# Relaying q, k and v through memory in runs of 64 floats instead of 16

## The reference

```
n  = layernorm(x)
q, k, v = n @ Wq.T, ctx @ Wk.T, ctx @ Wv.T      # each 16 heads x 16 channels, per token
attn = softmax(q . k * 0.25)                    # 16 x 16 head-by-head scores of one token
o  = attn . v, laid out as (head, token, channel) and read back as rows of 256
x  = x + o @ Wp.T + bp
x  = x + moe(layernorm(x)) + shared_ffn(layernorm(x))   # 16 experts, the best 2 per token
```

## Time and profile before

| what | us |
|---|---|
| median of three runs | 1795.53 (1794.02 to 1797.23) |
| the profiled execution | 1800.4 |
| its span | 1798.6 |
| PE busy | 1513.8 (84% of the span) |
| DVE busy | 1326.2 (74%) |
| POOL busy | 1315.4 (73%) |
| ACT busy | 726.7 (40%) |

### The profile page before, as it was taken

How to read it: one execution, slowest core, us unless ns; L and a number is a source line. 1 busy time by engine, 2 the same in 40 slices (tenths; PEclk the granted TensorE clock), 3 DMA queues, 4 the chain that set the end, 5 groups by cost and what they waited for, 6 DMA issues and landing times.

```text
span 1798.6 us, 50791 instructions
## 1 busy us (share of the span) xinstructions
PE 1513.8 (84%) x17109; PEld 1320.3 (73%) x17110; DVE 1326.2 (74%) x3378; ACT 726.7 (40%) x1346; POOL 1315.4 (73%) x1253
## 2 busy tenths in 40 slices
PE   4699999999999999999999999976677676676774
PEld 4578888888878887888888888855566666665774
DVE  6677889787999899988998999875455555455553
ACT  3344454445444544454445444422133332233231
POOL 4277787778787877878787878767567777677676
PEclk9799999999999999999999999987788988889887
DMA  8788888888898889888988898845877765777773
GB/s 219 151 191 174 175 164 228 184 181 164 212 199 173 173 207 199 176 175 182 224 176 178 186 212 175 151 166 210 259 216 215 223 210 165 216 210 228 210 216 91
DMA packets 945835, 344.76 MB, mean 192 GB/s; under 512 B 824088, under 2 KB 898730, under 8 KB 940288
## 3 DMA queue, kind: packets, MB, share of 16 engines
q1 hardware_dynamic: 892464, 166.19, 51.7%
q0 software_dynamic: 33600, 92.91, 14.0%
q10 hardware_dynamic: 19728, 85.13, 13.0%
HBM read 200.37 MB, written 148.15 MB: 194 GB/s over the span
## 4 chain that ended last, share of the span: by engine, by line
PE 31%; issue 17%; SPq 16%; DVE 13%; another core or an unknown queue 7%; POOL 6%; DMA 5%; ACT 4%; DVEq 0%; POOLq 0%; ACTq 0%
SPq L276 6%; SPq L281 5%; SPq L289 4%; PE bank_z L1460 4%; PE bank_a L1193 3%; PE bank_y L1180 2%; PE bank_y L1178 2%; PE bank_a L1332 2%; PE bank_y L1179 2%; ACT xn L645 2%; PE bank_z L1178 2%; DMA w_sb<-q_dram 2%; DMA kv_dram<-w_sb 2%; PE bank_z L1180 2%
## 5 line engine op out<-in xcount | busy, mean ns | idle before, releaser
L410 POOL DMA_INDIRECT slots<-xn,slot_i x256 | 279.4, 1091 | 98.2 <-issue 55.0
L1132 DVE SCALAR_TENSOR_TENSOR v_area<-bank_y,tail,v_area 128x256 f32<-128x256 f32 x288 | 121.6, 478 | 155.6 <-PE bank_y L1180 68.2
L531 POOL DMA_INDIRECT sums<-v_area,tail x144 | 147.1, 1022 | 65.3 <-issue 33.5
L1178 PE MATMUL bank_y<-w_hi,xn_hi 128*128 x288 | 98.8, 343 | 110.9 <-POOL xn_lo L523 79.6
L531 POOL DMA_INDIRECT out<-v_area,tail x144 | 147.5, 1024 | 52.9 <-issue 35.6
L722 ACT ACTIVATE th<-bank_z 128x512 f32<-128x512 f32 x72 | 43.0, 598 | 297.5 <-PE bank_z L1460 141.1
L1178 PEld LDWEIGHTS bank_y<-w_hi,xn_hi 128*128 128x128 f32 x288 | 59.5, 206 | 127.6 <-issue 127.2
L419 POOL DMA_INDIRECT sums<-v_area,slot_i x128 | 128.1, 1000 | 33.2 <-issue 29.8
L1178 PE MATMUL bank_y<-wsh_out_hi,hid_hi 128*128 128x256 f32 x512 | 143.0, 279 | 1.3 <-POOL hid_lo L441 1.3
L1180 PE MATMUL bank_y<-wsh_out_hi,hid_lo 128*128 128x256 f32 x512 | 142.8, 279 | 0.0
L1179 PE MATMUL bank_y<-wsh_out_lo,hid_hi 128*128 128x256 f32 x512 | 142.7, 279 | 0.0
(11 more groups left out here) (229 smaller groups left out, 5381.1 us busy)
## 6 DMA issues: line engine op xcount, KB each, us to landing
k_area<-slots SPq DMA_DIRECT2D x288, 129.0 KB
v_area<-sums SPq DMA_DIRECT2D x288, 128.0 KB
kv_dram<-w_sb ACTq DMA_DIRECT2D x32, 1024.0 KB
x_sb<-in_x_in SPq DMA_DIRECT2D x32, 512.0 KB
ctx_sb<-in_ctx_t SPq DMA_DIRECT2D x32, 512.0 KB
q_dram<-q_sb ACTq DMA_DIRECT2D x32, 512.0 KB
k_area<-kv_dram SPq DMA_DIRECT2D x256, 64.0 KB
w_sb<-q_dram SPq DMA_DIRECT2D x256, 64.0 KB
```

The lines of the kernel that those rows point to most:

```text
L410: pool.indirect_dma_start(slots[j], bass.IndirectOffsetOnAxis(ap=slot_i[:, par, j, i:i + 1], axis=0), row_of[j][:, i, :], None).then_inc(S ...
L531: pool.indirect_dma_start(target, bass.IndirectOffsetOnAxis(ap=tail[:, r, t, 1 - j:2 - j].bitcast(u32), axis=0), y_ring[:, r, t, :], None, ...
L1132: st = nc.vector.scalar_tensor_tensor(out=y_ring[:, r, t, :], in0=Y[t // 2][:, t % 2 * C:(t % 2 + 1) * C], scalar=tail[:, r, t, j:j + 1], ...
L1178: mm(out, lhs_hi, rhs_hi, start=start, stop=False)
```

## The change

A run of four tokens of one batch now lies side by side, so that a piece of the relay is 64 floats, 256 bytes.

- A projection tile takes every fourth token: token `4 p + i` comes out on partition p of tile i. The stationary side of the projections is therefore read with a step of four floats, 16 bytes. `x_sb` is loaded to match, with four DMAs in place of one.
- ScalarE writes the tiles interleaved: k and v as `(16, 4, 16)`, so that each run of 16 floats is followed by that of the next token; q as `(256, 4)`, so that neighbouring floats belong to neighbouring tokens and each copy writes with a step of 16 bytes.
- k and v have a DRAM tensor each. k and q are stored by four DMAs each, of 32 partitions, which put the rows in the order that the reads want; v is stored by one.
- The 24 reads have 16 pieces per partition, of 64 floats. `k_diag` and `v_diag` have the eighth outside of the token. q stays interleaved, so the stationary side of the score matmuls (32 columns) is read with a step of 16 bytes.
- The waits count the new numbers of DMAs: 80 for k and v in place of 16, 64 for q, 64 for x.

```diff
@@ sync
+            def load_x_in(c):
+                rows = x_in[c].rearrange("(m t) i f -> i m t f", t=BPC)
+                for i in range(BPC):
+                    sp.dma_start(x_sb[32 * i:32 * i + 32, :, :], rows[i]).then_inc(S["x_in_done"], 16)
...
-                sp.wait_ge(S["kv_stored"], at(16, c, 16))
+                sp.wait_ge(S["kv_stored"], at(80, c, 80))
                 for src, t in eighths:
                     rows = slice(16 * t, 16 * t + 16)
-                    sp.dma_start(k_diag[rows, :, t % 4, :],
-                                 kv[src, :, :, 0, :].rearrange("n i (d g) -> d (n i) g", d=D)).then_inc(S["qk_read"], 16)
-                sp.wait_ge(S["q_stored"], at(16, c, 16))
+                    sp.dma_start(k_diag[rows, t % 4, :, :].rearrange("d (n a) g -> d n (a g)", a=BPC), k[src]).then_inc(S["qk_read"], 16)
+                sp.wait_ge(S["q_stored"], at(64, c, 64))
                 for src, t in eighths:
                     rows = slice(16 * t, 16 * t + 16)
-                    sp.dma_start(q_rows[rows, :, t // 4 * H:(t // 4 + 1) * H],
-                                 q[src].rearrange("n i (d h) -> d (n i) h", d=D)).then_inc(S["qk_read"], 16)
+                    sp.dma_start(q_rows[rows, :, t // 4, :], q[src]).then_inc(S["qk_read"], 16)
...
@@ scalar
+            def store_by_eighth(dram, rows, done):
+                by_i = dram.rearrange("(t i n) f -> i t n f", t=8, i=BPC)
+                for i in range(BPC):
+                    act.dma_start(by_i[i], rows[32 * i:32 * i + 32, :]).then_inc(S[done], 16)
...
-                    nc.scalar.activation(kv_sb[:, i, :], KV_BANKS[i][:, :], ACT.Copy).then_inc(S["kv_out"], 1)
+                    nc.scalar.activation(kv_by_tile[:, i], KV_BANKS[i][:, :].rearrange("p (w o f) -> p w o f", w=2, f=H),
+                                         ACT.Copy).then_inc(S["kv_out"], 1)
-                act.dma_start(kv_dram[c], kv_sb).then_inc(S["kv_stored"], 16)
+                store_by_eighth(k_dram[c], kv_sb[:, 0:BPC * C], "kv_stored")
+                act.dma_start(v_dram[c], kv_sb[:, BPC * C:]).then_inc(S["kv_stored"], 16)
...
-                        st = nc.scalar.activation(q_sb[:, t, :], Q_BANKS[i][:, j * C:(j + 1) * C], ACT.Copy, scale=ln1_rstd[:, t:t + 1])
+                        st = nc.scalar.activation(q_by_tile[:, t], Q_BANKS[i][:, j * C:(j + 1) * C], ACT.Copy, scale=ln1_rstd[:, t:t + 1])
-                act.dma_start(q_dram[c], q_sb[:, :, :]).then_inc(S["q_stored"], 16)
+                store_by_eighth(q_dram[c], q_sb[:, :], "q_stored")
@@ tensor, scores
-                            m = (u * 8 + n) * BPC + QUARTER_OF[a]
-                            last = mm(SCORE_BANKS[u][32 * a:32 * a + 32, n * 4 * H:(n + 1) * 4 * H], q_rows[:, m, :],
-                                      k_diag[:, m, :, :].rearrange("p t g -> p (t g)"), start=True, stop=True)
+                            row, tile = QUARTER_OF[a] * 4 + u * 2 + n // 4, n % 4
+                            m = row * BPC + tile
+                            last = mm(SCORE_BANKS[u][32 * a:32 * a + 32, n * 4 * H:(n + 1) * 4 * H], q_by_row[:, row, tile, :],
+                                      k_diag[:, :, m, :], start=True, stop=True)
@@ tensor, project
-                        tokens = slice(i * P, (i + 1) * P)
+                        tokens = slice(i, TOK, BPC)
```

More of the change, by code:

```diff
@@ L59, in xattn_ffn_kernel @@
         q_dram = nc.dram_tensor("q_dram", [CHUNKS, P, BPC * C], f32).ap()
-        kv_dram = nc.dram_tensor("kv_dram", [CHUNKS, P, BPC * 2 * C], f32).ap()
+        k_dram = nc.dram_tensor("k_dram", [CHUNKS, P, BPC * C], f32).ap()
+        v_dram = nc.dram_tensor("v_dram", [CHUNKS, P, BPC * C], f32).ap()
         slots = [nc.dram_tensor(f"slots{j}", [NO_TILE + P, ROW], f32).ap() for j in range(TOP)]
@@ L95, in xattn_ffn_kernel @@
         ctx_sb = sb("ctx_sb", [P, KT, TOK])
-        q_sb = sb("q_sb", [P, BPC, C])
+        q_sb = sb("q_sb", [P, BPC * C])
+        q_by_tile = q_sb[:, :].rearrange("p (f i) -> p i f", i=BPC)
         w2_sb = sb("w2_sb", [P, E * C])
-        kv_sb = w2_sb[:, 0:BPC * 2 * C].rearrange("p (i f) -> p i f", i=BPC)
-        q_rows = w2_sb[:, BPC * 2 * C:].rearrange("p (m h) -> p m h", h=32)
+        kv_sb = w2_sb[:, 0:BPC * 2 * C]
+        kv_by_tile = kv_sb.rearrange("p (w o i f) -> p i w o f", w=2, i=BPC, f=H)
+        q_rows = w2_sb[:, BPC * 2 * C:].rearrange("p (n c f) -> p n c f", c=2, f=BPC * H)
+        q_by_row = w2_sb[:, BPC * 2 * C:].rearrange("p (n f i) -> p n i f", i=BPC, f=2 * H)
         k_area = sb("k_area", [P, GROUPS * P])
         v_area = sb("v_area", [P, GROUPS * P])
-        k_diag = k_area[:, 0:GROUPS * 4 * H].rearrange("p (m t g) -> p m t g", m=GROUPS, t=4)
-        v_diag = v_area[:, 0:GROUPS * 4 * D].rearrange("p (m t d) -> p m t d", m=GROUPS, t=4)
+        k_diag = k_area[:, 0:GROUPS * 4 * H].rearrange("p (t m g) -> p t m g", m=GROUPS, t=4)
+        v_diag = v_area[:, 0:GROUPS * 4 * D].rearrange("p (t m d) -> p t m d", m=GROUPS, t=4)
         w1_sb = sb("w1_sb", [P, E * KT * HID])
@@ L261, in chunk @@
                     sp.wait_ge(S["ln1_step"], at(1, c, 1))
-                    sp.dma_start(x_sb[:, :, :], x_in[c + 1]).then_inc(S["x_in_done"], 16)
+                    load_x_in(c + 1)
                     sp.wait_ge(S["ctx_split"], at(1, c, 1))
@@ L288, in chunk @@
                         r = QUARTER_OF[i] * 2 + t2
-                        sp.dma_start(v_diag[16 * r:16 * r + 16, :, r % 4, :],
-                                     kv_t2[t2, :, i, 1, :].rearrange("m (g d) -> g m d", g=H)).then_inc(S["v_read"], 16)
-            sp.dma_start(x_sb[:, :, :], x_in[0]).then_inc(S["x_in_done"], 16)
+                        sp.dma_start(v_diag[16 * r:16 * r + 16, r % 4, :, :].rearrange("g (m i) d -> g m (i d)", i=BPC),
+                                     v[i, t2]).then_inc(S["v_read"], 16)
+            load_x_in(0)
             sp.dma_start(wq_sb, wq).then_inc(S["w_q"], 16)
@@ L305, in _ @@
             sp.wait_ge(S["s_full"], 2 * CHUNKS)
-            sp.wait_ge(S["kv_stored"], 16 * CHUNKS)
+            sp.wait_ge(S["kv_stored"], 80 * CHUNKS)
             sp.dma_start(w2_sb[:, :], w2).then_inc(S["w_experts"], 16)
@@ L573, in x_round @@
                 st.then_inc(S["x_hi_ready"], 1)
+            def store_by_eighth(dram, rows, done):
+                by_i = dram.rearrange("(t i n) f -> i t n f", t=8, i=BPC)
+                for i in range(BPC):
+                    act.dma_start(by_i[i], rows[32 * i:32 * i + 32, :]).then_inc(S[done], 16)
             def project_out(c, first):
                 if not first:
[L577 to L578 removed]
+                    act.wait_ge(S["kv_stored"], at(80, c, 0))
+                    act.wait_ge(S["q_stored"], at(64, c, 0))
                 for i in range(BPC):
                     act.wait_ge(S["kv_full"], at(4, c, i + 1))
[L581 removed]
+                    nc.scalar.activation(kv_by_tile[:, i], KV_BANKS[i][:, :].rearrange("p (w o f) -> p w o f", w=2, f=H),
+                                         ACT.Copy).then_inc(S["kv_out"], 1)
                 act.wait_ge(S["kv_out"], at(4, c, 4))
[L583 removed]
+                store_by_eighth(k_dram[c], kv_sb[:, 0:BPC * C], "kv_stored")
+                act.dma_start(v_dram[c], kv_sb[:, BPC * C:]).then_inc(S["kv_stored"], 16)
                 act.wait_ge(S["ln1_pow"], at(1, c, 1))
@@ L755, in ln1_moments @@
             def ln1_moments(c, first):
-                dve.wait_ge(S["x_in_done"], at(16, c, 16))
+                dve.wait_ge(S["x_in_done"], at(64, c, 64))
                 for i in range(BPC):
@@ L1246, in project @@
                     for j in range(2):
-                        t = 2 * i + j
-                        tokens = slice(t * P, (t + 1) * P)
+                        tokens = slice(2 * i + j, TOK, BPC)
                         for k in range(KT):
@@ L1333, in attend @@
                                       prob_t[:, 32 * g:32 * g + 32],
-                                      v_diag[:, pair * 16 + u * 8 + n, :, :].rearrange("p t d -> p (t d)"), start=True, stop=True)
+                                      v_diag[:, :, pair * 16 + u * 8 + n, :], start=True, stop=True)
                     last.then_inc(S["o_full"], 1)
```

8 lines of the change are left out of this document (3 added, 5 removed).

## The result

| | us, median | runs |
|---|---|---|
| before | 1795.49 | 4 (1794.02 to 1797.23) |
| after | 1944.81 | 4 (1940.87 to 1950.91) |

The ratio is 1.0828, with a 95% interval from 1.0803 to 1.0852. The change makes the kernel 149 us slower. The forecast said 1786 and its range ended at 1838, so direction, size and range were all wrong. The ratios, here and in the experiments, leave out executions more than 1.5% above the fastest of the same kernel, which concerns e12 alone.

What follows compares the result with a forecast made beforehand. VectorE's loop was taken to bound it, 30.7 us of a 36.24 us period, TensorE close beside. Start -7.4, x issues +1.4, waits -6, ACT's queue +3 sum to -9.0: from 1795.5 to 1786 us, range 1768 to 1838.

Steps and rivals of the forecast that it cites:

- The relay: SP's DMA reads: longer pieces cut them from 9,780 to 3,930 us of engine time, a large relief hardly on the path.
- start and waits: Earlier q, v and scores at the start, -7.4 us; DMA waits of scores and VectorE after 100 us, -6.
- The start: First scores, first attend and second scores wait less for DMAs: -7.4 us; three more issues of x: +1.4.
- TensorE, "I take nothing": Stationary operands read with a step of 16 bytes: taken at no cost, with twice per column as upper bound.
- rival 1: Strided weight loads double in projections and scores: period +2.9 us, +90 in all, about 1876; chance 0.11.
- the third: The prediction's wording for the rival that bounds TensorE's strided loads at twice per column, which is rival 1.
- ACT's queue, "+0.1 us a chunk": Seven more issues a chunk on ACT delay tanh and residual rows: +3 us over 28 chunks, at most 42.
- The residual rows: Their load, issued 1.7 to 2.3 us later on ACT, lands in 4.3 us, near 462.8; wanted at 462.65.
- The rule weighed: SBUF lines of 16 bytes: crossing costs a penalty, yet four fp32 values are called free; rows silent on TensorE.

Runs made afterwards that it cites:

- e12: Kernel after, with packed projections (stationary side read side by side) and the residual's load issued ahead of ACT's copies and stores: 1910.3 us, ratio 1.0569.
- e4: Kernel after, with packed projections, the eight k and q stores issued by SP, and x in one load: 1780.2 us, ratio 0.9926.
- e2: Kernel after, with its eight k and q stores issued by SP in place of ACT: 1856.5 us, ratio 1.0354.
- e1: Kernel after, with tokens laid out by the host so that the projections read the stationary side packed: 1933.9 us, ratio 1.0782.
- e3: Kernel after, with q relayed in pieces of 16 floats as before the change: 1932.0 us, ratio 1.0767.
- e9: Kernel after, with the residual's load issued by ACT ahead of the copies and stores: 1883.2 us, ratio 1.0509.
- e5: Kernel before, with its projections reading the stationary side with a step of 16 bytes: 1869.5 us, ratio 1.0432.
- e7: Kernel before, with kv and q each stored by ACT in four transfers of 32 partitions, rows in the changed kernel's order: 1948.0 us, ratio 1.0868.
- e6: Kernel before, with its projections reading the stationary side with a step of 8 bytes: 1796.7 us, ratio 1.0005.
- e8: Kernel before, with kv and q each stored by ACT in four transfers of 32 partitions, to neighbouring rows: 1885.0 us, ratio 1.0506.

## Why the prediction was wrong, point by point

- *The relay.* Right in mechanism, too large in size. The DMA waits before the scores went, and their relief was nearly off the path: e4, with the two costs out, is 13 us below the kernel before, where start and waits were forecast to bring 7.4 and 6. That is agreement with another kernel (SP issues its stores, x comes in one load), and no test of the sum. The first scores of e4 came at 43.4, as the text had it (about 43), and the second at 68.0 (near 69). But the DMA share of the stage, forecast near 0.6, is 0.69 in e4, where the period is as before; the 0.66 of the kernel after spreads the same transfers over a longer period. A piece of 256 bytes was taken at 20 ns with 20.8 as bound. If the rest of SP's queue still takes 5,100 us (x now comes in smaller pieces), the 11,726 us leave 34 ns for each of the 196,608 pieces. It cost nothing here, since this was off the path.
- *The start.* Wrong for the kernel after. The first scores came 7.2 us later and not 3.2 earlier. In the kernel after ACT rounds x transposed, whose load is issued behind those of x, at 14.13 us where it did so at 10.26. Only a part of that comes with the four loads of x: e2 has the same four and rounds at 11.28, e1, e3, e9 and e12 at 11.2 to 12.2. The rest of the 3.9 us is not explained. e3, with the eight stores on ACT, has its first scores at 49.8, and e2, with them on SP, at 46.9; so these stores cost the start some 3 us.
- *TensorE, "I take nothing".* The first failed step. The argument was that 0.76 ns a column leaves room for a step. It did not: the load went to 326 ns for 128 columns, which is +138 where rival 1 had +97, and q's projection alone grew by 24 x 0.12 = 2.9 us against 1.4 of room. e5 prices it at 76 us. (The upper bound of this item is rival 1; the text calls it the third.) Rival 1's mechanism, place and threshold were right for the projections, and it had 0.11. Its other half was too large: the scores took 0.23 us more, not 2.0.
- *ACT's queue, "+0.1 us a chunk".* The step that failed most. It used 0.47 to 0.6 us an issue, from transfers of 128 partitions; the new ones take 0.75 to 0.80 from one to the next. The copies of q were taken at nothing with +0.85 as bound and took +0.58 of their own (e1). The tanh was forecast to end 1.7 to 2.3 us late and starts 5.5 late. The upper bound of the item, 1.5 us a chunk, was built from the same price of an issue and so was no bound: e7, the stores alone, costs 4.8 us a chunk (41.06 for 36.27).
- *The residual rows.* Taken at 4.3 us to land once the DMA engines are emptier, and wanted 6.08 us behind their issue (456.57 to 462.65). VectorE got them 6.84 us behind the issue (594.76 to 601.60). The emptier DMA engines didn't help: with a DMA share of 0.66 to 0.69 and none of the eight stores on ACT, the load still lands 6.1 (e2) and 5.8 us (e4) behind its issue in the middle, where it took 5.9. Behind q's four stores it may take up to a us more; no row separates that. The rest of the lateness is that of the issue. Issuing the load first brings 57 us with slow loads (e9) and 38 without (e12).
- *The rule weighed.* The rows show that one value per 16 bytes costs on TensorE too: 188 ns packed, 194 with a step of 8 bytes, 326 with one of 16. The Trainium skill, page "SBUF — State Buffer", section "Door 1: The DMA port swizzle", has lines of 16 bytes and a penalty for each access that crosses to a new one; that sentence agrees with e5, while in e6, where twice as many reads cross as in packed ones, the whole load pays 6 ns. Its other sentence, that a step of four fp32 values is free, does not hold for weight loads here.
- *The range.* It ended at 1838, since rival 1 was given 0.11 and ACT's queue was bounded at 42 us. The bound came from issues of another shape than the new ones; at the 5.5 us that ACT's path grew by, the upper end would have been near 1950, by the estimate 1786 + 30 x 5.5.

## What to carry to other kernels

Price an added DMA by what its issue costs in the very shape that it will have, and on the engine that issues it: splitting one transfer from 128 partitions into four from 32 multiplied the issue time by six to nine here, and what stood behind it on that engine (a tanh, a load) paid for it at nearly one us for one. Look at single issues and not at their mean: it hid that plain ones are as cheap as the large one until they are held. Then follow the engine that waits: here a wait of 3 to 4 us on TensorE cost its length and 1.3 to 2.3 us of half clock behind it (e12, e7, e1). Keep at least two floats side by side in a stationary operand, and when two suspected costs lie beside each other, take both out in one run, since either alone may show almost nothing.

## What the runs showed of the hardware that was not expected

- A weight load of 128 columns of 4 bytes takes 188 ns side by side, 194 with a step of 8 bytes and 310 to 332 with one of 16. One of 32 columns takes 115 and 148.
- ACT copies with a step of 16 bytes on the output: two of 128 x 256 take 1.20 us where they took 0.84.
- A store issued by ACT from 128 partitions takes it 0.37 to 0.40 us. One from 32 partitions takes 0.68 with rows that step in memory (0.75 to 0.87 from one to the next). With plain rows the median is 0.33 for q and 0.42 for kv, and some take 2.0 (e8). On SP four loads of 32 partitions of x took 2.66 us for 0.40. The Trainium skill, page "Perfetto Trace Analysis", section "What "DMA-bound" means", calls that window descriptor generation and not data movement. The rows agree that it isn't the bytes: a store of 512 KB (line 597, 0.39) took less than one of 128 KB (line 585, 0.68). No run shows why some plain ones are held.
- The granted clock fell to 0.50 at or just behind idle stretches of 3 to 4 us of PE (e1, e7, e12), and not in the kernel after, where slower work filled most of the same wait. In a window from 200 to 1200 us it is 1.00 before and after, 0.96 in e1 and 0.95 in e7 and e12.
